# Attention head pairs on one Trainium2 core: one output projection per two heads, turned reciprocals, and the q/k split on GpSimd

## What is computed

```python
q, k, v = (x @ W).reshape(B, T, H, dh)...        # W in (Wq, Wk, Wv); B=2, T=1024, H=16, dh=64
logits = (einsum('bhqd,bhkd->bhqk', q, k) + causal + pos_bias) / dh
probs = softmax(logits, axis=-1)
out = einsum('bhqk,bhkd->bhqd', probs, v)
return out.transpose(0, 2, 1, 3).reshape(B, T, H * dh) @ Wo + bo
```

## Time and profile before

| what | before |
|---|---|
| median of 3 runs | 845.11 us (845.06 to 845.23) |
| the profiled execution, its own time | 844.46 us |
| its span | 842.7 us |
| mean granted TensorE clock | 0.975 of full speed |
| PE busy | 771.5 us, 92% |
| DVE busy | 707.7 us, 84% |
| ACT busy | 612.8 us, 73% |
| POOL busy | 298.9 us, 35% |

### The profile page before, as it was taken

One profiled execution on the slowest core, in us unless ns is written; L12 is line 12 of the kernel. 1 busy time (PEld: TensorE's weight loads), 2 busy tenths in 40 slices (PEclk: granted clock), 3 DMA queues, 4 the chain that ended last, 5 costly groups with the idle time before them and its releaser, 6 DMA issues.

```text
span 842.7 us, 17198 instructions
## 1 busy us (share of the span) xinstructions
PE 771.5 (92%) x4436; PEld 657.1 (78%) x4436; DVE 707.7 (84%) x1596; ACT 612.8 (73%) x1340; POOL 298.9 (35%) x323
## 2 busy tenths in 40 slices
PE   3877999999999999999999999996489999999992
PEld 2656988888888888888889888885377777777771
DVE  5557888988888888888888888888778888898976
ACT  2356888887888888888788888873577767667672
POOL 2318823333332332333233233223503354445423
PEclk9899999999999999999999999999679999999997
DMA  7684334424423432442443343230003211122101
GB/s 279 219 280 89 75 66 97 88 62 87 100 62 76 95 77 62 93 94 62 87 95 67 70 97 82 62 75 26 25 1 129 76 60 43 46 75 75 51 1 50
DMA packets 56025, 70.72 MB, mean 84 GB/s; under 512 B 36032, under 2 KB 45120, under 8 KB 52544
## 3 DMA queue, kind: packets, MB, share of 16 engines
q1 hardware_dynamic: 55712, 69.83, 32.9%
q10 hardware_dynamic: 288, 0.59, 0.3%
HBM read 27.36 MB, written 9.50 MB: 44 GB/s over the span
## 4 chain that ended last, share of the span: by engine, by line
PE 75%; DVE 8%; issue 6%; POOL 4%; ACT 3%; DMA 3%; POOLq 0%; DVEq 0%; ACTq 0%; SPq 0%
PE out_ps L1191 16%; PE score_ps L1158 16%; PE trans_ps L1173 15%; PE shared_ps L1205 6%; PE trans_ps L1074 3%; PE score_ps L1074 3%; PE score_ps L1076 2%; PE score_ps L1075 2%; PE trans_ps L1075 2%; PE trans_ps L1076 2%; DVE pT_lo L961 2%; PE shared_ps L1074 2%; PE shared_ps L1076 2%; PE shared_ps L1075 2%; POOL rstd L421 1%
## 5 line engine op out<-in xcount | busy, mean ns | idle before, releaser
L649 ACT ACTIVATE probs<-score_ps,row_min 128x128 f32<-128x128 f32 (+7 forms) x256 | 189.9, 742 | 53.5 <-DVE row_min L848 53.4
L861 DVE TENSOR_TENSOR pT_lo<-trans_ps,pT_hi 128x512 fp32r<-128x512 f32 (+3 forms) x384 | 201.6, 552 | 16.7 <-ACT pT_hi L670 16.6
L670 ACT ACTIVATE pT_hi<-trans_ps 128x512 fp32r<-128x512 f32 (+3 forms) x384 | 185.1, 491 | 40.4 <-PE trans_ps L1173 28.8
L848 DVE CUSTOM_DVE_ANT_0 score_ps<-score_ps,bias 128x128 f32<-128x128 f32 (+7 forms) x256 | 194.6, 760 | 22.8 <-PE score_ps L1158 19.4
L1173 PE MATMUL trans_ps<-ident,probs 128*128 128x128 f32 x1152 | 190.0, 274 | 3.2 <-DVE pT_lo L861 1.8
L1158 PE MATMUL score_ps<-k_hl,q_hl 128*128 128x512 f32 (+2 forms) x768 | 182.5, 351 | 3.1 <-DMA k_hl<-k_hl 1.6
L470 POOL TENSOR_TENSOR acc<-acc,head_out 128x512 f32<-128x512 f32 x64 | 83.0, 1297 | 245.5 <-DVE head_out L879 245.3
L1173 PEld LDWEIGHTS trans_ps<-ident,probs 128*128 128x128 f32 x1152 | 136.8, 140 | 27.3 <-DVE pT_lo L861 11.9
L1191 PE MATMUL out_ps<-pT_hi,v_hl 128*128 128x512 f32 (+2 forms) x384 | 156.5, 409 | 1.1 <-DVE pT_lo L861 1.1
L961 DVE TENSOR_TENSOR pT_lo<-probs,pT_hi 128x512 fp32r<-128x512 f32 x144 | 133.2, 952 | 25.0 <-ACT pT_hi L728 15.1
L1158 PEld LDWEIGHTS score_ps<-k_hl,q_hl 128*128 128x128 f32 x768 | 134.4, 189 | 23.7 <-DMA k_hl<-k_hl 1.8
(11 more groups left out here) (122 smaller groups left out, 1163.3 us busy)
## 6 DMA issues: line engine op xcount, KB each, us to landing
q_hl<-k_hl SPq DMA_DIRECT2D x64, 256.0 KB, 3.6
k_hl<-k_hl SPq DMA_DIRECT2D x32, 512.0 KB, 4.2
v_scratch<-probs SPq DMA_DIRECT2D x16, 512.0 KB, 4.0
v_raw<-v_scratch SPq DMA_DIRECT2D x32, 256.0 KB, 4.6
bias_all<-gate_scratch SPq DMA_DIRECT2D x8, 1024.0 KB, 4.8
v_raw<-in_Wfc SPq DMA_DIRECT2D x8, 256.0 KB, 4.9
bias<-in_Wproj SPq DMA_DIRECT2D x8, 256.0 KB, 5.3
bias_all<-in_rel_steps SPq DMA_DIRECT2D x1, 1920.0 KB, 12.7
```

The lines of the kernel that those rows point to most:

```text
L649: act.activation(probs[s % 4][:, 0:n], scores_of(s % QB)[:, 0:n], ACT.Exp, bias=row_min[:, s:s + 1], scale=-1.0, accum_out=row_sum[:, s:s ...
L670: act.activation(pT_hi[c][:, CH * g:CH * g + m, q * P:(q + 1) * P], trans_ps[k % 2][:, 0:m * P].rearrange("p (m q) -> p m q", q=P), ACT.Co ...
L848: dve.tensor_tensor_reduce(out=ps, in0=ps, in1=bias_b[b][:, T - n:T], scale=1.0, scalar=3e38, op0=ALU.add, op1=ALU.min, accum_out=row_min[ ...
L861: dve.tensor_tensor(pT_lo[c][dst], trans_ps[k % 2][:, 0:m * P].rearrange("p (m q) -> p m q", q=P), pT_hi[c][dst], ALU.subtract).then_inc(p ...
```

## The change

**One projection per pair.** `o_pair[b][c]` is 128 x 512 and holds the even head in partitions 0 to 63 and the odd head in 64 to 127. ACT copies the other half of `out_ps` into the head's own half of `o_pair` (`copy_other`), DVE adds the own half from `out_ps` (`sum_halves`, slots 10, 14 and 2, 6 of the next head). When the odd head is there, POOL multiplies the pair by its reciprocals (`normalise_pair`, same slots), PE projects once (slots 12, 15 of the odd head, 4, 7 of the next), and DVE adds the result from `shared_ps` to `acc` (`add_pair`). `scale_head` and `add_head` are gone. The loop now does an odd and an even head per turn.

**Reciprocals.** In `o_pair` the tokens lie along the row. So DVE inverts in slots 4, 8, PE turns the four columns to four rows (`turn_inv`, one transpose in slots 6, 10, and 14, 2), ACT copies the 4 x 128 out (`copy_inv`), SP stores the rows of 512 bytes in DRAM (`store_inv`) and loads them spread over 64 partitions (`load_inv`).

**q and k.** ACT now only copies `shared_ps` to `qk_raw`; POOL makes `hi` and `lo`. `split_qk_lo` on DVE is gone.

```diff
-    PV1 = [11, 11, 11, 12, 13, 13, 14, 14]
-    WO = [11, 15]
+    PV1 = [11, 11, 12, 12, 12, 13, 13, 13]
+    WO = [12, 15]
+    SUM = [10, 14]
+    INV = [4, 8]
+    TURN = [6, 10]
...
+            def iteration(h, m, odd):                       # SP
+                if not first:
+                    load_inv(h - 1, 1, 0, m, not odd)
+                    sp.wait_ge(v_ready, h * B)
+                load_v(h, 1)
+                place_q(h, 1)
+                if not first:
+                    store_inv(h - 1, 1, 1)
+                    load_inv(h - 1, 1, 1, m, not odd)
+                place_k(h, 1)
+                if not last:
+                    sp.wait_ge(v_ready, h * B + 1)
+                    load_v(h + 1, 0)
+                store_inv(h, 0, 0)
+                load_inv(h, 0, 0, m, odd)
+                store_inv(h, 0, 1)
+                if not last:
+                    place_q(h + 1, 0)
+                load_inv(h, 0, 1, m, odd)
+                if not last:
+                    place_k(h + 1, 0)
+                store_inv(h, 1, 0)
...
+            def split_qk(h, b, half):                       # POOL
+                pool.wait_ge(qk_raw_ready, n + 1)
+                pool.tensor_copy(k_hl[b][:, 0, cols], qk_raw[half][:]).then_inc(qk_hi, 1)
+                pool.wait_ge(qk_hi, n + 1)
+                pool.tensor_tensor(k_hl[b][:, 1, cols], qk_raw[half][:], k_hl[b][:, 0, cols],
+                                   ALU.subtract).then_inc(qk_lo, 1)
+            def normalise_pair(m, b, c):                    # POOL
+                pool.wait_ge(inv_loaded[b][c], m * 32)
+                pool.wait_ge(o_summed, (m * 2 - 1) * (B * NC) + b * NC + c + 1)
+                pool.tensor_tensor(o_pair[b][c][:], o_pair[b][c][:], inv_all[b][c][:], ALU.mult).then_inc(o_ready, 1)
...
+            def sum_halves(h, b, c, odd):                   # DVE
+                dve.wait_ge(o_copied, h * (B * NC) + b * NC + c + 1)
+                dve.tensor_tensor(own_half, out_ps[half_of(odd), :], own_half, ALU.add).then_inc(o_summed, 1)
...
             def values(h, b, c, j0, j1):                    # PE
-                        pe.wait_ge(oT_ready, u)
+                        pe.wait_ge(o_summed, u)
...
             def project_out(m, b, c, j0, j1):               # PE
-                    pe.wait_ge(oT_ready, h * (B * NC) + b * NC + c + 1)
+                    pe.wait_ge(o_ready, (m - 1) * (B * NC) + b * NC + c + 1)
```

More of the change, by code:

```diff
@@ L173, in transformer_block @@
                      for i in range(2)]
-        gated = [head_out[c] for c in range(2)]
+        gated = [o_pair[0][c] for c in range(2)]
         acc_T = acc[:].rearrange("p t d -> p (t d)")
@@ L353, in _ @@
             load_v(0, 0)
-            head(0)
-            with sp.Fori(1, H - 1) as h:
-                head(h)
-            head(H - 1, last=True)
+            in_order(sp, iteration)
+            load_inv(H - 1, 1, 0, PAIRS, True)
+            store_inv(H - 1, 1, 1)
+            load_inv(H - 1, 1, 1, PAIRS, True)
             def load_expert(i, wf, wp):
@@ L524, in _, with iteration @@
             split_v(0, 0)
-            for s in range(S):
-                slot(0, s, False, False)
-            with pool.Fori(1, H - 1) as h:
+            def iteration(h, m, odd):
                 for s in range(S):
-                    slot(h, s, True, False)
-            for s in range(S):
-                slot(H - 1, s, True, True)
+                    slot(h, s, not (isinstance(h, int) and h == 0), isinstance(h, int) and h == H - 1, m, odd)
+            in_order(pool, iteration)
             def split_wfc(e, i):
@@ L605, in nT_evac, with evacuate_qk @@
                    .then_inc(nT_hi_ready, 1)
-            def split_qk_hi(h, b, half):
+            def evacuate_qk(h, b, half):
                 act.wait_ge(qk_psum, h * (2 * B) + 2 * b + half + 1)
-                if not (isinstance(h, int) and h == 0):
-                    act.wait_ge(scores_ready, h * S + QB * b + QB - S)
-                act.activation(k_hl[b][:, 0, half * W:(half + 1) * W], shared_ps[:], ACT.Copy).then_inc(qk_hi, 1)
+                if not (isinstance(h, int) and h == 0 and b == 0):
+                    act.wait_ge(qk_lo, h * (2 * B) + 2 * b + half + 1 - NC)
+                act.activation(qk_raw[half][:], shared_ps[:], ACT.Copy).then_inc(qk_raw_ready, 1)
             def copy_v(t):
@@ L693, in slot, with iteration @@
                     if not (nxt and last):
-                        split_qk_hi(h + nxt, b, half)
-            for s in range(S):
-                slot(0, s, False, False)
-            with act.Fori(1, H - 1) as h:
+                        evacuate_qk(h + nxt, b, half)
+            def iteration(h, m, odd):
                 for s in range(S):
-                    slot(h, s, True, False)
-            for s in range(S):
-                slot(H - 1, s, True, True)
+                    slot(h, s, not (isinstance(h, int) and h == 0), isinstance(h, int) and h == H - 1, m, odd)
+            in_order(act, iteration)
             def normalise_moe_in(b):
@@ L884, in slot, with invert_sums @@
-            def slot(h, s, carried, last):
+            def invert_sums(h, b, c):
+                u = h * (B * NC) + b * NC + c
+                rows = slice(QB * b + CH * c, QB * b + CH * (c + 1))
+                if not (isinstance(h, int) and h == 0):
+                    dve.wait_ge(inv_evac, u - B * NC + 1)
+                    dve.sem_inc(dve_passed, 1)
+                dve.wait_ge(probs_ready, h * S + QB * b + CH * c + CH)
+                dve.reciprocal(row_inv[:, rows], row_sum[:, rows]).then_inc(inv_ready, 1)
@@ L885, in slot @@
+            def slot(h, s, carried, last, m, odd):
                 row_minimum(h, s)
+                for n, before, b, c in own_and_carried(SUM_SLOT, s, h):
+                    sum_halves(n, b, c, odd != before)
                 if s >= LAG_DVE:
```

308 lines of the change are left out of this document (175 added, 133 removed).

## The result

| what | before | changed |
|---|---|---|
| median of 4 runs each | 845.09 us (844.28 to 845.23) | 947.63 us (943.02 to 954.63) |
| ratio to before | 1 | 1.122, 95% interval 1.115 to 1.129 |
| the profiled execution, its span | 844.46, 842.7 us | 943.02, 941.2 us |
| PE, DVE busy | 771.5, 707.7 us | 784.5, 700.9 us |

The forecast was 886 (+41), the range 856 to 912. Slower was right; the size was not: +102.5. It lies outside every rival.

What follows compares the result with a forecast made beforehand. The prediction took PE to bound the kernel (479.5 of 495 us busy). Head 0's 14, the halves' 19.5 and the tail's 7.6 us made +41 on 844.46, 885.6; with the median 0.65 higher, 886 (range 856 to 912).

Steps and rivals of the forecast that it cites:

- Head 0: Head 0 and the half behind it: POOL, splitting v first, delivers q and k late; 14 us (10 to 16).
- The tail: Behind the last scores: multiply, projection and add follow POOL's roots, +4.4 and +3.2 us; together 7.6 (4 to 10).
- The halves: Heads 2 to 15 and head 1's second half: +2.7 us a pair, 19.5 us in all (1 to 44).
- Time from E to the first scores: From slot 9's q/k projection end (E) to next half's scores: 11.51 us before; PE's way 10.55 without projections, 12.33 with.
- it is not the bound: DVE in the attention: it sheds 44 and 42 us, takes 42 and 21, so it does not set the time.
- E to SP's q issue: From the q/k projection's end in slot 9 (E) to SP issuing q: about 3.0 us instead of 1.7.
- For batch 1: SP's queue: a reciprocal store, then a load waiting for it, stand before k; about 1.1 us late (0.3 to 2.1).
- The term for the reciprocals in slot 7: Even head's first half: the pair's last projection waits for POOL, which waits for the reciprocals' load; +1.2 us (+0.8 to +2.9).
- PE's busy time: PE over the kernel: busy time falls by 20 us and the time rises all the same.
- Short detours: Rival: SP's detours are short, out_ps is free in time, head 0 overlaps better; +15 to 20, about 862 us; chance 0.22.
- POOL against DVE: Rival: they contend in the attention at the experts' prices; 21 us more, 907, up to 914 us; chance 0.10.
- PE stays the bound: Rival: q and k have over 2 us more slack, so the kernel gets faster; 837 us, 825 at best; chance 0.08.

Runs made afterwards that it cites:

- e10: The changed kernel with DVE's addition of a half's first projection one slot later, and head 0's q and k split by ACT and DVE: 943.9 us.
- e11: The kernel before with only the change's two slot tables, for v products and output projections: 878.0 us, ratio 1.040.
- e13: The changed kernel without DVE's sums of halves and without the reciprocals (additions of own halves and division by row sums left out): 890.2 us.
- e6: The changed kernel without inversion, turn, copy, store and load of reciprocals (division by row sums left out): 911.9 us.
- e1: The kernel before with two heads in each turn of the hardware loop, nothing else changed: 866.8 us, ratio 1.028.
- e2: The changed kernel with the loop over pairs written out as Python, so no jump back: 940.8 us.
- e14: The changed kernel with SP moving k before it stores and loads reciprocals: 1009.3 us.
- e5: The changed kernel with the split of q and k given back to ACT and DVE: 978.3 us.
- e9: The changed kernel with DVE's addition of a half's first projection one slot later and the loop over pairs written out: 940.1 us.

## Why the prediction was wrong

**Head 0** (+14 forecast): +15.5, with its times. But when ACT and DVE split q and k in head 0 (e10), only 7 to 8 of these 15.5 us come back. The other half has causes that the forecast did not name, and no run separates them; so the fit is in part luck.

**The tail** (+7.6): +7.3 behind the last row minimum, +7.9 behind the last scores, where some 8 were forecast. The steps are the forecast ones, DVE standing for PE's projection twice:

```profile
678.44 0.69 DVE L977 TENSOR_TENSOR acc<-shared_ps,acc 128x512 f32<-128x512 f32 x1 [5.30 <-PE shared_ps L1312]
...
689.13 2.05 PE L1312 MATMUL shared_ps<-wo,o_pair 128*128 128x128 f32 x8 [10.02 <-POOL o_pair L553]
691.33 0.69 DVE L977 TENSOR_TENSOR acc<-shared_ps,acc 128x512 f32<-128x512 f32 x1 [5.29 <-PE shared_ps L1312]
```

The parts are off and cancel: to the first `newton` +6.5 where 4.4 was forecast, behind it +0.7 where 3.2 was. The last projection takes 2.05 us where 1.0 was forecast: PE stood for 10.0 us before it, and the granted clock is at the lower level from 684.1 to 701.2 us.

**The halves** (+19.5): +73.5 in the 28 behind head 1's first and +3.4 in the last one, together +76.9. Here the prediction failed, in three steps.

1. *"Time from E to the first scores ... PE's own way: without projections 11.51 - 1.78 + 0.22 + 0.6"*. This adds PE's work over a half as though PE set every slot. It nearly did, before (97% busy); that is a property of where the work stood, and the two tables that moved it were costed at nothing and not named. They cost 1.1 us a half and 33.5 us in all (e11), more than the whole sum forecast for the halves. The 1.78 us that PE sheds in halves without projections are worth 1.0 (17.7 to 16.7 in e13).
2. *"DVE sheds 44 and 42 us, takes 42 and 21; it is not the bound."* A busy share of 74% hides it. In slots 6 and 7 DVE's row minimum and `split_lo` already fill the slot before the sum is added. The forecast had only the wait for `out_ps` (0.6 us a half; measured 17.9 us in 31 waits, 0.58 each, and about right). The delay of `split_lo` was missing, and with it 19 us of PE's waits at the transposes (1.8 in e13, 21.2 in e6). From e13 to e6 the sums cost 0.65 us in slot 6 alone, and in all 0.9 to 1.2 us in a half with projections, nothing in one without.
3. The loop's length: "The loop now does an odd and an even head per turn" stood in the text as a fact without a price. DVE's six stands there lengthen six halves by 3.2 us, 19 us in all, and alone the longer loop costs 22 (e1); writing it out in the changed kernel gives back only 7 (e2), since the halves of odd heads grow.

The terms behind them were about right in kind. k: E to SP's q issue was forecast 3.0 and is 3.85 (q at 487.25 for a projection that ends at 483.4; ACT's copy starts at E+0.98 instead of E+0.35), E to the k issue over 8: 9.0 (at 492.34). For batch 1 SP issues k 0.7 to 0.9 us behind the landing of q, as forecast (0.8), and the move then takes 4.9 to 5.4 us, 1.0 more than for batch 0, where its share of the forecast was 0.3. For batch 0, where 0.3 us was forecast, there is nothing: k goes 0.02 us behind q and lands in 4.1. The term for the reciprocals in slot 7 (1.0 us in the first half of even heads) is nothing either: that half takes 18.6 us without them (e6) and 18.7 with them. PE does wait for k, but on most halves it is late itself and the wait is short; the long ones are where the projections are missing. That is so in the first halves of odd heads: their 1.6 us over e6 make 11 us in seven heads, some 1.0 of the 1.6 from SP's detour (e14).

**PE's busy time** did not fall by 20 us, it rose by 13. By the groups of its instructions the output projections fell by 34.5 us (70.0 to 35.5), the turns took 17.7 (0.28 us each, where 0.11, the distance between two in a row, was forecast), scores and transposes took 15 more, and the other groups of the attention 6 less. That is 8 us less by groups, and 13 more by the page's total, which counts overlapping groups once. As I read it, less overlaps where PE stops and starts, so busy time is a poor measure of what a pipelined engine sheds; no run tried that.

**The rivals.** Short detours (862): refuted by k's path for batch 1 above, and by e14. POOL against DVE (907 to 914): POOL's subtract takes 1.29 us in the changed kernel, as the split of v before; refuted. PE stays the bound (837): refuted by the windows.

**The ledger.** Measured on the kernel before: tables 33.5, q and k on POOL 29.1. Measured by leaving them out of the changed kernel: reciprocals and sums together, with the jump, 57.4. That is 120, and 103 were measured. The two first parts alone would give 844.6 + 62.6 = 907.2, and e13 is 890.2, so 17 us come back there. That the ledger closes shows nothing, since the 17 is what the subtraction leaves. PE's lighter work in half of the halves is the likely source. The projection per pair without the rest of the change was not run, and e5 shows that these parts do not simply add.

## What to carry to other kernels

Where three engines pass each slot on to the next in a hand-written order, read each slot's length against each engine's work in it before moving anything. Work taken from an engine pays only in slots where that engine is the slowest; work added pays nothing only where it is not. A table entry that only moves work is a term of the sum like any other. And an improvement that makes a loop body longer has to be read against the instruction queue: a packet count on the profile's page that rises with the turns of a loop tells that its body is fetched again.

## What was not expected of the hardware

- A loop body of 279 or 290 DVE instructions is fetched again at each jump back, about 3 us each, 46 to 47 packets on the instruction queue in all; one of 266 is not (17 packets).
- During waits of PE of only 2 us, or up to 1.1 us behind them, the granted clock fell to the lower level, six times in e2, each for 3.4 us or more. Each fall cost about 1.5 us (e9), nearly as much again as the wait. In the changed kernel waits of the same length passed without one.
- The same edit had opposite signs in the two kernels: the split of q and k on GpSimd, +29 us alone, -31 us within the change.
